# Attention and a mixture of experts on one core: setup and turns reordered, biases added at read-out, feed-forward begun mid-turn, score maxima laid as rows by DMA through DRAM

## The reference

```python
q = (x1 @ Wq + bq).reshape(Bn, Nq, H, D).transpose(0, 2, 1, 3)      # 16 heads of 16
k = jnp.concatenate([x2 @ Wk + bk, memory_k], axis=1)
v = jnp.concatenate([x2 @ Wv + bv, memory_v], axis=1)
attn = jax.nn.softmax(jnp.einsum('bhqd,bhkd->bhqk', q, k) * scale, axis=-1)
out = jnp.einsum('bhqk,bhkd->bhqd', attn, v) ... @ Wp + bp
x = x + out
# then 8 experts over every token, 256 -> 1024 -> 256
h = jax.nn.silu(x @ w_gate[e]) * (x @ w_up[e])
out = sum over e of (h @ w_down[e]) * cw[:, e]        # cw: two softmaxes over the experts
x = x + out
```

## Time and profile before

| | us |
|---|---|
| median of 3 runs | 2844.45 (2843.43 to 2844.73) |
| profiled execution, its own time | 2842.41 |
| its span in the profile | 2840.6 |

### The profile page before, as it was taken

How to read it: one execution, slowest core, us unless ns; L and a number is a source line. 1 busy time by engine, 2 the same in 40 slices (tenths; PEclk the granted TensorE clock), 3 DMA queues, 4 the chain that set the end, 5 groups by cost and what they waited for, 6 DMA issues and landing times.

```text
span 2840.6 us, 47444 instructions
## 1 busy us (share of the span) xinstructions
PE 2754.5 (97%) x16512; PEld 2248.5 (79%) x16512; DVE 2151.3 (76%) x3218; ACT 1702.8 (60%) x3313; POOL 1686.0 (59%) x1612
## 2 busy tenths in 40 slices
PE   5789999999999999999999999999999999999998
PEld 3567888888887888888888887888888888887887
DVE  4787787878878787787878778787787777766665
ACT  4776666666666666665666666666666665544443
POOL 2655666556666566666566666565666655554554
PEclk8899999999999999999999999999999999999999
DMA  1002232232322323232232322223222233333332
GB/s 56 31 20 86 82 97 86 79 112 86 98 89 83 104 86 94 90 97 94 75 101 93 102 88 84 92 90 105 82 90 86 79 108 91 102 105 112 104 103 83
DMA packets 250715, 251.76 MB, mean 89 GB/s; under 512 B 15848, under 2 KB 242288, under 8 KB 250480
## 3 DMA queue, kind: packets, MB, share of 16 engines
q1 hardware_dynamic: 250480, 248.73, 28.6%
HBM read 240.15 MB, written 8.52 MB: 88 GB/s over the span
## 4 chain that ended last, share of the span: by engine, by line
PE 86%; DVE 7%; ACT 3%; issue 3%; POOL 1%; SPq 0%; DMA 0%; POOLq 0%; ACTq 0%; DVEq 0%
PE ps_t L617 23%; PE ps_s L617 23%; PE ps_o L651 22%; PE ps_s L714 4%; PE ps_t L723 3%; PE ps_m L513 2%; PE ps_a L694 2%; PE ps_a L696 2%; DVE Pt_lo L1039 1%; PE ps_m L551 1%; DVE hf L911 1%; PE ps_m L521 1%; PE ps_m L558 1%; PE ps_m L566 1%; DVE css L973 1%
## 5 line engine op out<-in xcount | busy, mean ns | idle before, releaser
L916 DVE TENSOR_TENSOR h_lo<-hf,h_hi 128x512 fp32r<-128x512 f32 x512 | 545.5, 1065 | 323.0 <-ACT h_hi L742 317.6
L742 ACT ACTIVATE h_hi<-hf 128x512 fp32r<-128x512 f32 x512 | 323.5, 632 | 574.3 <-DVE hf L911 571.4
L904 DVE SCALAR_TENSOR_TENSOR hf<-hf,ps_s 128x512 f32<-128x512 f32 x512 | 349.8, 683 | 255.1 <-ACT hf L737 251.6
L1182 POOL TENSOR_TENSOR Pt_lo<-Pt 128x512 f16<-128x512 f32 x256 | 285.6, 1116 | 432.3 <-ACT Pt L870 431.4
L737 ACT ACTIVATE hf<-ps_s 128x512 f32<-128x512 f32 x512 | 306.2, 598 | 300.4 <-PE ps_s L617 161.1
L1121 POOL TENSOR_TENSOR wd_lo<-stage_w,wd_hi 128x512 fp32r<-128x512 f32 x256 | 338.1, 1321 | 139.5 <-ACT wd_hi L749 139.0
L1121 POOL TENSOR_TENSOR wg_lo<-stage_w,wg_hi 128x512 fp32r<-128x512 f32 x256 | 337.1, 1317 | 137.2 <-ACT wg_hi L749 137.2
L651 PE MATMUL ps_o<-h_hi,wd_hi 128*128 128x512 f32 x1024 | 399.4, 390 | 0.9 <-DVE h_lo L916 0.9
L651 PE MATMUL ps_o<-h_lo,wd_hi 128*128 128x512 f32 x1024 | 399.6, 390 | 0.0
L651 PE MATMUL ps_o<-h_hi,wd_lo 128*128 128x512 f32 x1024 | 398.7, 389 | 0.0
L1092 DVE TENSOR_REDUCE negmax<-ps_s 128x1 f32<-128x512 f32 x512 | 346.8, 680 | 31.4 <-PE ps_s L714 27.4
(11 more groups left out here) (189 smaller groups left out, 5121.7 us busy)
## 6 DMA issues: line engine op xcount, KB each, us to landing
stage_w<-in_L_ffn_w_gate_dram SPq DMA_DIRECT2D x256, 256.0 KB, 2.7
stage_w<-in_L_ffn_w_up_dram SPq DMA_DIRECT2D x256, 256.0 KB, 2.9
stage_w<-in_L_ffn_w_down_dram SPq DMA_DIRECT2D x256, 256.0 KB, 2.7
cwb<-d_cw SPq DMA_DIRECT2D x64, 256.0 KB, 3.5
X<-in_x_dram SPq DMA_DIRECT2D x32, 256.0 KB, 3.0
C<-in_fside_BxSxS_dram SPq DMA_DIRECT2D x16, 256.0 KB, 3.4
VF<-in_ctx_dram SPq DMA_DIRECT2D x16, 256.0 KB, 3.0
d_x<-X SPq DMA_DIRECT2D x16, 256.0 KB, 3.1
```

The costliest lines, as they stand in the source:

```text
L742: act.activation(h_hi[f % FC][:], hf[:], ACT.Copy).then_inc(hh_done, 1)
L904: dve.scalar_tensor_tensor(out=hf[:], in0=hf[:], scalar=1.0, in1=ps_g[:], op0=ALU.add, op1=ALU.mult).then_inc(gate_done, 1)
L916: dve.tensor_tensor(h_lo[f % FC][:], hf[:], h_hi[f % FC][:].bitcast(F32), ALU.subtract).then_inc(hl_done, 1)
L1182: pool.tensor_tensor(Pt_lo[slot][:], Pt[slot][:], Pt[slot][:].bitcast(BF16)[:, 1::2], ALU.subtract).then_inc(lo_pool.sem, 1)
```

## The change

Six things change together.

1. **Setup.** Inputs of the first batch are loaded first, then the weights in the order in which they are needed; PE, ACT and DVE wait for each when they need it. ACT makes the high parts, POOL clears the tiles. The first turn has its own places for four items.
2. **Biases** are added by DVE where it reads a projection out of PSUM (`kv` and `q`, which ACT read out before), and for `o` by POOL into the residual beforehand. The L507 products are gone.
3. **Score maxima** go as `mq` (128 partitions by 8 values) by a DMA into DRAM `d_mq` and come back by two DMAs as rows of 256 into `QTs`. The PE transposes (L558) and the ACT copies (L841) are gone; `qq` becomes `qT`.
4. **AHEAD** is 10.
5. **Feed-forward** starts at step 19 of turn 2 (START = 83 steps after turn 0 begins, 96 before). The last turn is 18, and the banks are joined from that step on.
6. **Items, statistics and router work** have other places in the turn; the end of a group (`y`) comes at steps 23 and 25, and X2 has a tile of its own.

```diff
-    AHEAD = 8
+    AHEAD = 10
+    START = GB * STEPS + 19
+    CLOSED = START // STEPS + GB
+    d_mq = nc.dram_tensor("d_mq", [2, 2, 4, P], F32, kind="Internal").ap()
...
+        ITEMS = [(0, "qT", 3, 0), (1, "kT", 4, 0), (2, "kT", 5, 0), (3, "cT", 0, 1), (4, "qT", 4, 0), (5, "aT", 0, -1),
...
+        FIRST_AT = {"cT": (1,), "kv": (3, 7), "xT": (5,), "q": (9,)}
...
@@ sync @@
+                    d, i = item_at(step, AHEAD - 2)
+                    if turn.has(d) and i % 4 == 3:
+                        pair = i // 4
+                        turn.wait(eng, mq_l, d, pair + 1)
+                        turn.wait(eng, qm_in[pair % 2], d, 32 * (pair // 2))
+                        eng.dma_start(d_mq[pair % 2].rearrange("s c q -> q s c"), mq[:, pair % 2].bitcast(F32),
+                                      allow_slow_non_contiguous=True).then_inc(mq_out.sem, 16)
+                    d, i = item_at(step, AHEAD - 4)
+                    if turn.has(d) and i % 4 == 3:
+                        pair = i // 4
+                        turn.wait(eng, mq_out, d, 16 * (pair + 1))
+                        for h in range(2):
+                            top = HS * h + 2 * HD
+                            eng.dma_start(QTs[top:top + 2, pair % QRING, h, :].bitcast(F32),
+                                          d_mq[pair % 2, :, 2 * h:2 * h + 2].rearrange("s t q -> s (t q)")).then_inc(qm_in[pair % 2].sem, 16)
@@ tensor @@
-                if bias is not None:
-                    pe.matmul(ps[:, col:col + width], minus_one[:], brow[:, bias].rearrange("p b n -> p (b n)"),
-                              start=True, stop=False)
...
-                    if turn.has(d):
-                        turn.wait(pe, mq_l, d, k + 1)
-                        for t in range(QT):
-                            mm = pe.transpose(ps[:, t * P:(t + 1) * P].bitcast(F32R), mq[k % 2][:, t, :], ident_r[:])
...
                         if kc == 0:
-                            turn.wait(pe, qm_done, 0, 2 * pair + 2)
+                            turn.wait(pe, qm_in[pair % 2], 0, 32 * (pair // 2 + 1))
@@ scalar @@
-                            for h in range(2):
-                                top = slice(HS * h + 2 * HD, HS * h + 2 * HD + 2)
-                                act.activation(QTs[top, k % QRING, h, :], ps[top, 0:N], ACT.Copy).then_inc(qm_done.sem, 1)
@@ vector @@
+                    if name == "kv":
+                        dve.tensor_tensor(KVM[:, k:k + QT + 1:QT, :], ps[:].rearrange("p (s n) -> p s n", n=D), bias[:, 1:3, :],
+                                          ALU.add).then_inc(kv_done.sem, 1)
```

More of the change, by code:

```diff
@@ L314, in one_bank @@
-        def one_bank(turn, banks, i):
-            return banks[0] if turn.ffn else banks[i % 2]
-        def octet_bank(turn, o):
-            return ps_a[:] if turn.ffn or o % 2 else ps_o[:, 0, :]
-        def wait_read_out(eng, turn, count, d, i):
-            turn.wait(eng, count, d, i if turn.ffn else i - 1)
-        ORDER = [sum(item[1] != "y" for item in MISC[:n]) for n in range(len(MISC))]
-        def bank(turn, n):
-            return ps_o[:, 1, :] if ORDER[n] % 2 and not turn.ffn else ps_m[:]
@@ L332, in wait_bank @@
-        def wait_bank(eng, turn, n):
-            same = [m for m in range(len(MISC)) if turn.ffn or MISC[m][1] != "y" and (ORDER[m] - ORDER[n]) % 2 == 0]
-            earlier = [(Turn(turn.b - 1), m) for m in same] + [(turn, m) for m in same if m < n]
-            for then, m in reversed(earlier):
-                freed = released(then, *MISC[m][1:])
-                for counter, value in freed:
-                    eng.wait_ge(counter, value)
-                if freed:
-                    return
+            return [(count.sem, (b + d) * count.per + nth)] if turn.has(d) else []
@@ new lines, in items_of @@
+        def items_of(b):
+            present = [(s, name, k, d) for s, name, k, d in ITEMS if released(b, name, k, d)]
+            if b == -1:
+                present = [(FIRST_AT[name][k] if name in FIRST_AT else s, name, k, d) for s, name, k, d in present]
+            return sorted(present)
+        items, last_in = {}, {}
+        for b in range(-2, LAST + 1):
+            for step, name, k, d in items_of(b):
+                joint = b * STEPS + step >= START
+                one = joint or len(items) % 2 == 0
+                items[b, step] = (name, k, d, one, last_in.get(one, []))
+                last_in[one] = released(b, name, k, d)
+                if not joint:
+                    last_early = dict(last_in)
@@ new lines, in misc, with bank, wait_all, score_bank @@
+        def misc(turn, step):
+            return items.get((turn.b, step), (None, None, None, None, None))
+        def bank(one):
+            return ps_m[:] if one else ps_o[:, 1, :]
+        def wait_all(eng, freed):
+            for counter, value in freed:
+                eng.wait_ge(counter, value)
+        def score_bank(j):
+            return ps_s[0] if j - AHEAD >= START else ps_s[j % 2]
+        def wait_scores_read(eng, j):
+            wait_for(eng, max_done.sem, j if j - AHEAD >= START else j - 1)
@@ new lines, in key_bank, with wait_keys_read, octet_in_a, octet_bank @@
+        def key_bank(j):
+            return ps_t[0] if j >= START else ps_t[j % 2]
+        def wait_keys_read(eng, j):
+            wait_for(eng, exp_done.sem, j if j >= START else j - 1)
+        def octet_in_a(o):
+            return o % 2 == 1 or o * OCT + OCT + 3 >= START
+        def octet_bank(o):
+            return ps_a[:] if octet_in_a(o) else ps_o[:, 0, :]
+        def octet_before(o):
+            return next((m for m in range(o - 1, -1, -1) if octet_in_a(m) == octet_in_a(o)), -1)
@@ L811, in body @@
                         high_of(f + 1)
-                    n, name, k, d = misc(turn, step)
-                    ps = bank(turn, n) if name else None
+                    name, k, d, one, _ = misc(turn, step)
+                    ps = bank(one) if name else None
                     if name in ("xT", "cT", "aT", "x2T"):
@@ L869, in body @@
                         turn.wait(act, av_ps, 0, KC * (i // KC) - RING + KC)
-                        act.activation(Pt[i % RING][:], one_bank(turn, ps_t, i)[:], ACT.Exp).then_inc(exp_done.sem, 1)
-            turns(body, before_ffn, first_weights)
+                        if turn.b == 0 and i == 0:
+                            act.wait_ge(w_low, len(parts))
+                        act.activation(Pt[i % RING][:], key_bank(turn.b * STEPS + i)[:], ACT.Exp).then_inc(exp_done.sem, 1)
+            turns(body)
```

424 lines of the change are left out of this document (203 added, 221 removed), and 8 rows, old and new, of tables (ITEMS, MISC).

## The result

The changed kernel took **3094.5 us** (median of 4 runs, 3087.4 to 3097.5), the kernel before 2844.6 beside it (4 runs). The ratio is 1.088, its 95% interval 1.0868 to 1.0894: 250 us slower. The forecast of 2787 was wrong, and the time lies far outside its range. The profiled execution took 3091.6, its span is 3089.6 us.

What follows compares the result with a forecast made beforehand. PE's own queue was taken to bound steady turns, the chain between engines turns 0 and 1. Terms -32 - 7 - 15 - 3 = -57 took the profiled 2842.41 to 2785, plus 2.0 for the median: 2787 us, range 2769 to 2815.

Steps and rivals of the forecast that it cites:

- The trip through DRAM: Maxima out and back by DMA: write about 4 us, trip 8 to 10 us, hidden after the first pair: 0.
- The trip's place on SP: SP waits for the write before the DMAs in; two steady steps of 10.6 us cover its 4 us: 0.
- rival D: Write over two SP steps (10.6 us) delays weight loads and ACT, 107 us per us excess; about 2880 at 12; chance 0.07.
- Rival E: Trip late only in short steps before feed-forward, 1 to 2 us over in 20 pairs: about 2805 us; chance 0.06.
- The Trainium skill: Read-modify-write below 512 bytes speaks against the DRAM write; if it doubled a piece, out takes 8.8 us, under 10.6.
- PE work removed: Steady turns lose 16 transposes and 6 bias products on PE: 2.4 us a turn over 13.4 turns, -32 us.
- rival C: Beginning gains more and DVE's waits go: -19 setup, -8 turns 0 to 2, -6 waits, 2772 us; chance 0.12.
- Read-out: ACT loses copies, DVE gains 2.0 us a turn, POOL one pass; hidden under PE in steady turns: 0.
- rival B: DVE crowds at step 10 and PE waits, 1 to 2 us a turn: 2800 to 2814 us; chance 0.22.
- Setup, ramp and START: Beginning: setup -15 us, turns 0 to step 19 of turn 2 -3, feed-forward 13 steps earlier -7.

Runs made afterwards that it cites:

- a2: The kernel before, plus an unread DRAM write of 1024 pieces of 4 bytes a pair, SP waiting for it only ahead of the next write: 3103.9 us.
- b1: The changed kernel with maxima written as 128 pieces of 32 bytes and gathered back by four DMAs of 256 4-byte pieces each: 2799.5 us.
- a4: The changed kernel with the two DMAs into QTs issued one step later on SP: 3128.6 us.
- c2: The kernel before plus an unread write of 1024 4-byte pieces a pair, 512 bytes apart, SP waiting for its landing two steps on: 2843.7 us.
- c4: The kernel before plus an unread write of 128 adjacent 4-byte pieces a pair in one 512-byte row, SP waiting two steps on: 2916.0 us.
- f1: The changed kernel with 32-byte writes and 4-byte gathers of the maxima (b1), and DVE's router work moved behind the hidden values' low part (d3): 2773.1 us.
- d3: The changed kernel with PE transposes instead of the DRAM trip (a1), and DVE's router work moved behind the hidden values' low part: 2801.1 us.
- a1: The changed kernel with the DRAM trip undone: PE transposes and ACT copies of the maxima are back, all other parts kept: 2831.5 us.

## Why the prediction was wrong

- **The trip through DRAM** is the step that failed. It took the write at 4 us, between 2.2 and 5.5, from the price of a 1 KB packet on 16 engines. It landed after 10.1, and from write to return it was 10.3. The upper bound was a bound on the engines' work, and the packets themselves are indeed short (7 to 9 ns), but what the landing waits for lies elsewhere and goes with addresses, which no row of the kernel before showed.
- **The trip's place on SP** failed second, and on its own. It asked only whether SP would stand longer than two steps, and set the turning point at 11.1 us. The write took less than that, and the kernel lost 250 us. The loads had been issued in time and were held in the queue behind it (10.7 us for the `gate` load at 1471.93; a2, whose steady turns have no wait of SP for the write, is as slow). The cover was too large besides: SP's two steps aren't 10.6 us but 8.6 (b1), so SP did stand, 90 times after 265 us; a4, with one such stand, shows that this isn't what costs. The place of the harm and its chain (weight loads, ACT, hidden values, PE) were those of rival D; its condition was wrong, and with it its chance of 0.07. By D's arithmetic a write of 10.3 us costs nothing. (A write of 12 us would cost (12 - 10.6) x 107 = 150 us by it and give 2937, not the 2880 that stands there.) Measured is 185.4 - 169.2 = 16.2 us a turn, 2.0 us a write (b1 against after), 13.4 x 16.2 = 217 us of the 295 between the two.
- **Rival E** (short steps) was right in kind and too small: not 1 to 2 us over in 20 pairs, but (84.4 + 86.4 - 55.7 - 60.2) / 16 = 3.4 us a pair in turns 0 and 1, since the write and return of neighbouring pairs form one chain on SP; SP stood for the write 187.9 us there, 21 times. With the first 19 steps of turn 2 the stage came out 73.5 us over the forecast.
- **The Trainium skill** ("DMA: Bandwidth & Descriptors", Specifications) speaks of a read-modify-write below 512 bytes. As a warning it pointed the right way, though no run shows such a read-modify-write. As a price it doesn't fit the runs: c2 writes 1024 pieces of 4 bytes and lands in 3.1 us, c4 writes 128 and lands in 8.0. A rule by the size of a piece can't tell them apart.
- **PE work removed** was right. In f1 a steady turn takes 167.2 us, 3.2 less than before, forecast -2.4; f1 and d3 differ by 169.2 - 167.2 = 2.0 us, which are the 16 transposes forecast at 8 x 0.19 = 1.5. Over 13.4 turns it makes -43, forecast -32. The rest is a small part of rival C: from 400 to 2400 us PE's waits for `hf` were 10.3 and 3.3 us in the kernel before and are 1.7 in f1, about 1 us a turn.
- **Read-out at 0 in the mean** was wrong by 2 us a turn, and rival B right in kind: b1 against f1 is 169.2 to 167.2, a1 against d3 171.5 to 169.2. The large passes that the forecast counted for step 10 did no harm; two tiny ones beside POOL's passes did.
- **Setup, ramp and START** hold where the write isn't in the way. In f1 the first score stands at 25.3 (forecast 25), the first `ps_t` at 37.8 (36), the first feed-forward product at 182.6 (183).

```profile
37.78 0.79 PE L752 MATMUL ps_t<-QTs,KTs 128*128 128x512 f32 x1 [2.09 <-DMA QTs<-d_mq]
...
182.61 0.70 PE L649 MATMUL ps_s<-xh,wg_hi 128*128 128x512 f32 x2 [0.73 <-ACT Pt L890]
```

With the write mended and the router's work moved, the kernel comes to within 2787 - 2773 = 14 us of the sum. That isn't the forecast come true, since neither edit is part of the change; b1, with the write mended alone, took 2799.5. The terms that had a size were good; the write, at nothing, cost 3094.5 - 2799.5 = 295 us (after against b1).

What stays open: why pieces that fill a row are slow, and what the unit is (64 adjacent pieces in a row weren't tried, only 64 at every second place); and why loads behind such a write move so few bytes. The Trainium skill ("DMA: Bandwidth & Descriptors", Queues, rings and completion order) says that the signal of a DMA's end lands only after every earlier write of the same DMA engine. The `gate` load that is reported late behind the write agrees with it, and the forecast should have weighed it; but the bytes were late too, not only their signal: 12 to 23 GB/s during the write and 287 after it, with each byte up to 4.9 times as long in an engine. So the order of the signals alone doesn't explain it.

## What to carry to other kernels

A transfer that is issued early can still be late: ask of each new DMA not only who waits for it, but which loads stand behind it in the queue and how much slack they have. When a transfer is made of tiny pieces, put them on the side of the read, or keep them from filling a stretch of DRAM one by one, and measure the landing before building on it: the share of busy DMA engines doesn't show a jam. And look for small passes of DVE between the two that PE waits for, above all beside POOL's; moving one such call gave 1.1% here.

## What the runs showed of the hardware that I had not expected

- A DMA of 4-byte pieces written to adjacent addresses in DRAM took 8.0 us for 128 pieces (c4) and 10.1 for 1024, while 1024 pieces at 8, 16 and 512 bytes took 4.6, 3.4 and 3.1 us; the 4-byte packets themselves show 7 to 9 ns.
- While it is under way, other loads in the same queue trickle: 12 to 23 GB/s, and 287 right after.
- Reading the same bytes in 4-byte pieces costs nothing that shows: f1, with 1024 such reads a pair, has 166432 packets under 512 bytes and PE busy all of its steady turns.
- A DVE pass over 128x2 values took 1.27 us beside a POOL pass of 1.30 us, and 0.15 where POOL was idle; one over 128x16 1.03 and 0.17 us. In both slow cases the DVE pass ended with POOL's, within 0.03 us.
